# First pass of a vision tower: scan decays made in pairs of steps, hidden layers in two runs, norm roots and gate scratch in PSUM, routing two steps later

## The chip, the cores and the metric

The kernel runs on one core of a Trainium2 chip, as one launch. The time is device time in microseconds (us), the median of several runs of the same program. The core has five engines that run at once and wait for each other by semaphores: TensorE (PE, with its weight loads, PEld), VectorE (DVE), ScalarE (ACT), GpSimd (POOL) and SyncE (SP, which here only issues transfers). SBUF is the on-chip memory of 128 partitions, PSUM the small one of eight banks that PE's products are written to.

## What is computed

32 images of 96x96 become 38 tokens each of 192 features: 36 patches and two class tokens. Two layers follow, each a state-space scan and a mixture of experts, both with a residual. Cut to what matters here, the first layer:

```
def mlp(x, w1, b1, w2, b2): return silu(x @ w1 + b1) @ w2 + b2

x = layernorm(h)                            # tokens x 192
a = -abs(mlp(x, A...)); b = mlp(x, B...); c = mlp(x, C...)      # 16 states each
delta = sigmoid(mlp(x, d...)); dt = exp(log_dt)                 # 192 each
# along the tokens of an image, for each feature and state:
state = (delta * state + (1 - delta) * x * b * dt) * exp(a * dt)
y = sum over states(state * c) + x * D
h = h + y
logits = layernorm(h) @ Wr.T                # 8 experts
top 2 of 8, weights = softmax of the two
h = h + sum over the two: weight * (gelu(x @ Wi[e].T + bi[e]) @ Wo[e].T + bo[e])
```

The second layer has two selective scans (forward and backward) between a projection down and one up, and a second mixture whose gates are chosen in the same way.

## The kernel before

The images are cut into four groups of eight, so T = 304 token columns. Features lie on partitions, 128 of them ("main", names ending in m) and 64 ("rest", ending in r). Some tensors pack both parts as PK = 456 columns, the rest's two halves of 152 columns under each other.

**Three stages.** The first pass does the first layer's scan and the routing of its experts; 34 expert blocks follow (they begin while the last group is scanned); the second pass does the second layer. The change lies in the first pass, and in two helpers that the second pass uses too.

**The first pass** is software pipelined. A body (s, p, m) scans group s, prepares group p and routes group m, and the program runs six: (none, 0, none), (0, 1, none), (1, 2, 0), (2, 3, 1), (3, none, 2), (none, none, 3). Each body has twelve steps n = 0 to 11 (QSTEPS), and for every engine a function `first(s, p, m)` says by hand what it does in step n: the order of work is that of the code, and engines meet by semaphores alone. In the text p and m are also the groups' buffers (p_Xm is group p's normed main part; m's centred parts lie in q_Cm and q_Cr).

**Scan of s**, one step for each of twelve slices of states and features, tiles of 128x608: SP loads decays dA and b rows BB into a ring of four slots; ACT makes the exponentials `exp(a*dt)` with `p_decay` (L996, two of 304 columns) into a ring EXq of EXPS = 3 buffers, two steps ahead (AHEAD); POOL multiplies dA by them (L719); DVE does the b product into PSUM (L1298), the c product (L1311) and the scan (L1319); POOL multiplies scan and c product (L725); PE sums that over states (`first_sum`). The c product of step c waits for the sum of step c - 3 (ring PR3). At the end of a body the states C, A and B of the next group come from PE's `states` and ACT (L1070 to L1075).

**Preparing p**: `patches` and `tokens` make the tokens (class columns copied on DVE, L1350, patches added, L1352). `centre` takes the mean off (L1202, L1203), ACT squares (L880, L882), PE's `variance` sums them, `rstd` makes the root as logarithm (L887) and exponential (L892) into RS, and DVE's `scale` multiplies (L1207, L1208). Eleven hidden layers follow (PE, then a silu on ACT, L921), in order 3, 3, 3, 2 over steps 2 to 5; the first two belong to the delta. ACT's `delta` makes the sigmoid (L1013, L1015). Then DVE's `first_scan_input` (step 5):

```
OM = -1 * DL + 1                                  # L1363
WV = (OM * dt0) * UP, main and rest apart         # L1365
DL[first token of each image] = 0, then signal w_ready
base = x * D0 + h, three parts                    # L1369
```

UP is a copy of x made by ACT (L1058 to L1060).

**Routing m**: mean, variance, root and scale as above (scale at step 4), logits on PE and ACT, `gates_top` (step 8) picks the two best experts with comparisons and maxima of 102x24 (L1224 to L1238), `ranks` on PE counts the tokens before each one, `route` and `give_slots` (step 9) make weights and slots (L1264 to L1280), POOL scatters the rows to their slots. After groups 1 and 3 `make_table` (L1498 to L1521, step 10) makes the table of expert blocks. The scratch of the gates lies in SBUF (m_gate, m_gs, KEEP). ACT loads a table of functions each time it changes between the silu, the sigmoid and the exponential/logarithm (ACT_TABLE_LOAD).

**Queues of the transfers.** SP's queue has the ring's loads in order of the steps, the stores of the group before and, in the scan of group 3, from step 4 on, the weights and rows of the first expert blocks. These also wait for the table and for the scatters of POOL's queue.

**The second pass** norms and chooses gates with the same `scale`, `gates_top` and `gates_weights` (L1242 to L1256).

## Time and profile before

| | |
|---|---|
| median of 3 runs | 945.74 us (945.5 to 946.44) |
| the profiled execution | 946.11 us, span 944.3 us |
| mean granted TensorE clock | 0.899 of full speed |
| busy, share of the span | PE 741.0 us (78%), PEld 62%, DVE 576.6 (61%), ACT 404.1 (43%), POOL 386.8 (41%) |
| instructions | 11558 |
| first bodies | 0 to 54 us prepare group 0 and load constants |
| scans of groups 0, 1, 2 | 54 to 108, 108 to 175, 175 to 247 us |
| scan of group 3, with the first expert blocks | from 247 us |
| second pass | from 534 us |

How to read it: a share of busy time is a mean over stages that have different limits. A stretch says how busy each engine was in it; the groups by line say how long one instruction of a kind takes and how long its engine stood idle just before it, with the instruction that ended that idle time; the timeline lists single instructions with their start. Busy time of PE is modelled. Three views can show the same microsecond: an idle time of DVE is also a busy or an idle time of the engine it waits for.

### The profile page before, as it was taken

How to read it: one execution, taken by the hardware profiler on the slowest of the kernel's cores; microseconds unless marked ns; L12 is line 12 of the kernel's file. 1: busy time of each engine (PE TensorE's matmuls, PEld its weight loads, DVE VectorE, ACT ScalarE, POOL GpSimd, SP SyncE). 2: the span in 40 equal slices, each digit the busy share in tenths (PEclk: the TensorE clock that was granted, in tenths of full speed). 3: DMA queues.
4: the chain of work that ended last, by engine and by line, in shares of the span. 5: the costliest groups of instructions: out<-in, count | busy, mean ns of one | idle time of the engine just before them, and what ended most of it. 6: DMA issues, size and time to landing. Idle time of an engine off the chain costs nothing. (4 is left out here: it accounts for less than half of the span.)

```text
span 944.3 us, 11558 instructions
## 1 busy us (share of the span) xinstructions
PE 741.0 (78%) x3622; PEld 585.7 (62%) x3622; DVE 576.6 (61%) x994; ACT 404.1 (43%) x875; POOL 386.8 (41%) x305
## 2 busy tenths in 40 slices
PE   7877888685547869877999677888886997787688
PEld 5645656454327869877898545666664775565455
DVE  4167779679765532312111387899796859777835
ACT  1549275374233324422245373644724455355120
POOL 1045745655672411303003144654366433653430
PEclk9899999798677989999999888888977999899899
DMA  9469755355494658888677597787679565967600
GB/s 353 128 205 343 228 154 152 91 136 142 127 266 113 185 170 242 254 258 232 191 241 223 152 233 190 195 220 189 158 201 252 151 168 143 268 167 187 195 1 21
DMA packets 84067, 177.66 MB, mean 188 GB/s; under 512 B 12671, under 2 KB 32357, under 8 KB 83365
## 3 DMA queue, kind: packets, MB, share of 16 engines
q1 hardware_dynamic: 79172, 169.67, 63.6%
q0 software_dynamic: 4832, 7.24, 2.6%
q8 instruction: 29, 0.48, 0.2%
q14 instruction: 34, 0.27, 0.1%
HBM read 156.15 MB, written 20.69 MB: 187 GB/s over the span
## 5 line engine op out<-in xcount | busy, mean ns | idle before, releaser
L1759 PE MATMUL PS<-PR,CM 128*128 128x304 f32 (+1 forms) x672 | 186.8, 420 | 92.3 <-POOL PR L806 63.2
L806 POOL TENSOR_TENSOR PR<-ST,V 128x608 f32<-128x608 f32 x96 | 142.4, 1483 | 185.5 <-DVE ST L1340 153.8
L1759 PEld LDWEIGHTS PS<-PR,CM 128*128 128x128 f32 x672 | 126.8, 221 | 134.7 <-POOL PR L806 76.8
L976 ACT ACTIVATE dA<-dA,negA 128x304 f32<-128x304 f32 x192 | 93.7, 540 | 151.3 <-DMA BB<-rows_d 151.1
L1340 DVE TENSOR_TENSOR_SCAN ST<-dA,PS 128x608 f32<-128x608 f32 x96 | 136.4, 1420 | 15.1 <-ACT dA L976 11.0
L1028 ACT ACTIVATE HID<-PS,WX 128x128 f32<-128x128 f32 x204 | 59.6, 367 | 150.0 <-PE PS L1759 149.9
L719 POOL TENSOR_TENSOR dA<-dA,aP 128x607 f32<-128x607 f32 x48 | 70.7, 1474 | 71.5 <-ACT aP L996 69.7
L1536 DVE TENSOR_TENSOR xp<-PS,WXB 128x192 f32<-128x192 f32 x34 | 12.2, 358 | 127.0 <-PE PS L1759 127.0
L1329 DVE TENSOR_TENSOR PS<-BB,PS 128x608 f32<-128x608 f32 x96 | 76.2, 794 | 21.5 <-DMA BB<-rows_d 10.7
L1759 PE MATMUL PS<-XT,WX 128*128 128x128 f32 x408 | 83.3, 288 | 1.0 <-ACT HID L1028 1.0
L1759 PE MATMUL PS<-XT,WXR 128*128 128x128 f32 x408 | 83.0, 287 | 0.0
L734 POOL DMA_DIRECT2D outs_d<-xp x34 | 19.5, 573 | 147.9 <-DVE xp L1536 147.9
L1759 PE MATMUL PS<-WX,HID 128*128 128x192 f32 x408 | 74.1, 331 | 7.3 <-DVE XT L1529 7.3
L1759 PEld LDWEIGHTS PS<-WX,HID 128*128 128x128 f32 x408 | 67.5, 194 | 8.2 <-issue 4.8
L725 POOL TENSOR_TENSOR PR<-PR,ST 128x608 f32<-128x608 f32 x32 | 47.2, 1474 | 59.4 <-DVE ST L1319 59.3
L1319 DVE TENSOR_TENSOR_SCAN ST<-dA,PS 128x608 f32<-128x608 f32 x48 | 67.8, 1413 | 2.5 <-POOL dA L719 1.8
L1759 PEld LDWEIGHTS PS<-XT,WX 128*128 128x128 f32 x408 | 66.4, 204 | 1.2 <-ACT HID L1028 1.2
L1759 PEld LDWEIGHTS PS<-XT,WXR 128*128 128x128 f32 x408 | 66.0, 204 | 0.0
L1759 PE MATMUL PS<-HB,CM 96*128 96x152 f32 (+1 forms) x240 | 48.8, 355 | 0.2 <-ACT HB L1130 0.2
L1759 PEld LDWEIGHTS PS<-HB,CM 96*128 96x128 f32 x240 | 40.1, 204 | 8.1 <-issue 3.1
L1759 PE MATMUL PS<-p_Xm,WX 128*128 128x304 f32 x88 | 32.8, 456 | 14.5 <-ACT HID L921 11.6
L1298 DVE TENSOR_TENSOR PS<-BB,PS 128x608 f32<-128x608 f32 x48 | 38.0, 792 | 9.3 <-ACT PS L1075 7.1
(380 smaller groups left out, 1318.6 us busy)
## 6 DMA issues: line engine op xcount, KB each, us to landing
dA<-rows_d SPq DMA_DIRECT2D x144, 304.0 KB, 4.4
BB<-rows_d SPq DMA_DIRECT2D x144, 304.0 KB, 5.1
WX<-ex_m SPq DMA_DIRECT2D x34, 576.0 KB, 4.0
WX<-ex_m SPq DMA_DIRECT2D x34, 387.0 KB, 3.8
slots_d<-WXR SPq DMA_DIRECT2D x8, 960.0 KB, 8.8
WXR<-ex_r SPq DMA_DIRECT2D x34, 192.0 KB, 4.9
CM<-c SPq DMA_DIRECT2D x1, 4430.0 KB, 19.6
WX<-gates_d SPq DMA_DIRECT2D x3, 1216.0 KB, 6.6
```

The lines of the kernel that those rows point to most:

```text
L719: nc.gpsimd.tensor_tensor(now[:, 1:], now[:, 1:], before[:, 0:QB * T - 1], ALU.mult).then_inc(ap_ready.sem, 1)
L725: nc.gpsimd.tensor_tensor(PR3[c % 3], PR3[c % 3], STq[:, c % 2], ALU.mult).then_inc(P.product.sem, 1)
L734: pool.dma_start(outs_d[b // HALF_BLOCKS][at:at + 128, :], YB[:, b % 3, :]).then_inc(out_rows[b % 3], 16)
L806: nc.gpsimd.tensor_tensor(PRq[:, c % 2], STq[:, c % 2], DIRS[k].Cw.unsqueeze(1).broadcast_to([128, QB, T]), ALU.mult).then_inc(q_product.s ...
L976: last = nc.scalar.activation(dAq[:, slot, i, :], dAq[:, slot, i, :], ACT.Exp, scale=negA[:, j:j + 1])
L1028: last = nc.scalar.activation(HX[:, p, f, :], PS[:, wide_bank(b, h), j * 128:(j + 1) * 128], ACT.Gelu, bias=WX[:, p, FFN + f:FFN + f + 1])
L1298: nc.vector.tensor_tensor(BPq[0], BBq[:, slot], PS[:, B1_BANK, 0:T].unsqueeze(1).broadcast_to([128, QB, T]), ALU.mult).then_inc(P.b_times_ ...
L1319: nc.vector.tensor_tensor_scan(flat(STq[:, c % 2], False), flat(dAq[:, slot], False), BP[0], 0.0, ALU.mult, ALU.add).then_inc(P.scanned.se ...
L1329: nc.vector.tensor_tensor(BPq[k], BBq[:, slot], BW[k].unsqueeze(1).broadcast_to([128, QB, T]), ALU.mult).then_inc(b_times_w.sem, 1)
L1340: nc.vector.tensor_tensor_scan(flat(STq[:, c % 2], back), flat(dAq[:, slot], back), BP[k][:, ::-1] if back else BP[k], 0.0, ALU.mult, ALU. ...
L1536: nc.vector.tensor_tensor(YB[:, p, :], PS[:, SHARED_BANK, 256:256 + D], WXB[:, p, :], ALU.add).then_inc(y_copied.sem, 1)
L1759: return nc.tensor.matmul(out, lhsT, rhs, start=first, stop=last)
```

## The change

**Buffers.** EXPS becomes 6. The three new buffers of the decays lie over buffers that only the second pass uses: two in q_DL_OM_WV (DL, OM and WV of the second pass) and one in p_OM_TM; group p keeps DL and WV apart.

**Order on ACT.** In a middle body the decays come in pairs of steps (DECAYS_AT), those of steps 0 and 1 still at the end of the body before. Squares and root of p come ahead of the step's decays. The hidden layers come in two runs, 0 to 5 and 6 to 10, with the delta between them and no decays within a run.

**Delta.** ACT scales UP by dt0 as it copies. Beside the sigmoid DL it makes 1 - delta as sigmoid(-x - b), into the PSUM bank that holds the delta's product. DVE's `first_scan_input` multiplies UP by that bank: one product of 456 columns in the place of OM and two.

**Roots and gates.** `rstd` writes the root into the PSUM bank of the variance (except for one norm, L), and `scale` reads it there. The scratch of the gates lies in the same bank (`choice_views`); the copy of the logits goes, copies of the second choice and of the first weight come.

**Class tokens** are copied for group 0 only; the buffers keep them.

**Routing** comes later where a group is prepared in the same body (`routed_at`): scale of m at step 6 for 4, logits 7 for 5, transposed logits 8 for 7, gates 9 for 8, route and slots 10 for 9, the table 11 for 10. POOL's scatters follow.

**Order on PE.** The variance of p comes before the sum of step 0, layers 0 and 1 before the mean of m, the delta's product after four layers, and at the end of a body the states B before the sum of step 10. Patches and token rows wait for WV (w_ready) instead of the delta.

The core of the diff:

```diff
-SLOTS, AHEAD, EXPS = 4, 2, 3
+SLOTS, AHEAD, EXPS = 4, 2, 6
+DECAYS_AT = {0: (2, 3), 1: (4, 5), 2: (6, 7), 4: (8, 9), 6: (10, 11)}
...
+        def routed_at(n, p):
+            if p is None or n <= 3:
+                return n
+            return {6: 4, 7: 5, 8: 7, 9: 8, 10: 9, 11: 10}.get(n)
...
             def rstd(s, g, bank):
                 act.wait_ge(s.ln_var.sem, s.ln_var.after(g, 1))
                 log_of(s, 128, bank, s.ln_log)
-                power_of(s, 128, s.ln_log, s.ln_rstd, g, 1)
+                power_of(s, 128, s.ln_log, s.ln_rstd, g, 1, None if s is L else PS[:, bank, 0:T])
...
-                nc.scalar.activation(P.DL[:, T:PK], PS[:, MEAN_BANK, T:PK], ACT.Sigmoid, bias=cm("d_b2", 1, 2)).then_inc(delta_ready.sem, 1)
+                nc.scalar.activation(P.DL[:, T:PK], PS[:, MEAN_BANK, T:PK], ACT.Sigmoid, bias=cm("d_b2", 1, 2))
+                for h, cols in enumerate(MAIN_REST):
+                    tables[0] = None
+                    last = nc.scalar.activation(PS[:, MEAN_BANK, cols], PS[:, MEAN_BANK, cols], ACT.Sigmoid, bias=neg_db2[:, h:h + 1], scale=-1.0)
+                last.then_inc(delta_ready.sem, 1)
...
+                    for c in DECAYS_AT.get(n, ()) if s is not None else ():
+                        p_decay(s, c)
...
-                            nc.scalar.activation(P.UP[:, 0:T], P.Xm[:, :], ACT.Copy)
+                            nc.scalar.activation(P.UP[:, 0:T], P.Xm[:, :], ACT.Copy, scale=dt0[:, 0:1])
...
-                        if n == 4:
-                            hidden(p, 6, 9)
                         if n == 5:
-                            hidden(p, 9, 11)
+                            hidden(p, 6, 11)
...
-            def scale(s, g, li):
+            def scale(s, g, li, bank):
                 dve.wait_ge(s.ln_rstd.sem, s.ln_rstd.after(g, li + 1))
-                nc.vector.tensor_tensor(s.Xm[:, :], s.Cm[:, :], s.RS[:, :], ALU.mult)
+                nc.vector.tensor_tensor(s.Xm[:, :], s.Cm[:, :], PS[:, bank, 0:T], ALU.mult)
...
+            def choice_views(bank):
+                each = TILES * EXPERTS
+                wide = [PS[0:TW, bank, T + j * each:T + (j + 1) * each].rearrange("p (t e) -> p t e", e=EXPERTS) for j in range(6)]
...
-                link(s, g, nc.vector.tensor_copy(L, PS[0:TW, bank, 0:TILES * EXPERTS].rearrange("p (t e) -> p t e", e=EXPERTS)))
...
+                    link(s, g, nc.vector.tensor_copy(oh2, picked))
...
-                    nc.vector.tensor_copy(hv[:, :, 0:2], cm(cls, p=rows).unsqueeze(1).broadcast_to([rows, IMG, 2]))
+                    if g == 0:
+                        nc.vector.tensor_copy(hv[:, :, 0:2], cm(cls, p=rows).unsqueeze(1).broadcast_to([rows, IMG, 2]))
...
-                link(P, g, nc.vector.tensor_scalar(P.OM[:, :], P.DL[:, :], -1.0, 1.0, ALU.mult, ALU.add))
-                for h, cols in enumerate(MAIN_REST):
-                    nc.vector.scalar_tensor_tensor(P.WV[:, cols], P.OM[:, cols], dt0[:, h:h + 1], P.UP[:, cols], ALU.mult, ALU.mult)
+                nc.vector.tensor_tensor(P.WV[:, :], P.UP[:, :], PS[:, MEAN_BANK, 0:PK], ALU.mult)
...
-                    pe.wait_ge(delta_ready.sem, delta_ready.after(p - 1, 1))
+                    pe.wait_ge(P.w_ready.sem, P.w_ready.after(p - 1, 1))
```

**ACT, the first steps of the body that scans group 1.** Before (L996 decays, L880 and L882 squares of p, L887 and L892 its root, L859 and L921 table loads, HID and HIDr the silus, aP the ring of decays):

```order
L880 ACTIVATE p_RS<-p_Cm 128x304
L882 ACTIVATE p_SQr<-p_Cr 64x304
L996 ACTIVATE aP<-q_R,neg_dtq 128x304 x2
L887 ACTIVATE p_VE<-PS,eps_col 128x304
L892 ACTIVATE p_RS<-p_VE 128x304
L996 ACTIVATE aP<-q_R,neg_dtq 128x304 x2
L921 ACT_TABLE_LOAD
L921 ACTIVATE HID<-PS,WX 128x304
L921 ACTIVATE HIDr<-PS,WX 64x304
L921 ACTIVATE HID<-PS,WX 128x304
L859 ACT_TABLE_LOAD
L996 ACTIVATE aP<-q_R,neg_dtq 128x304 x2
```

With the change (L1009 decays, L893 and L895 squares, L900 and L905 the root, now into PS; q_DL_OM_WV and p_OM_TM are the new buffers of the ring):

```order
L893 ACTIVATE p_RS<-p_Cm 128x304
L895 ACTIVATE p_SQr<-p_Cr 64x304
L1009 ACTIVATE aP<-q_R,neg_dtq 128x304 x2
L1009 ACTIVATE q_DL_OM_WV<-q_R,neg_dtq 128x304 x2
L900 ACTIVATE p_VE<-PS,eps_col 128x304
L905 ACTIVATE PS<-p_VE 128x304
L1009 ACTIVATE q_DL_OM_WV<-q_R,neg_dtq 128x304 x2
L1009 ACTIVATE p_OM_TM<-q_R,neg_dtq 128x304 x2
L1009 ACTIVATE aP<-q_R,neg_dtq 128x304 x4
L934 ACT_TABLE_LOAD
L934 ACTIVATE HID<-PS,WX 128x304
L934 ACTIVATE HIDr<-PS,WX 64x304
```

The decays of step 3 and those of steps 4 to 7 stand around the root, then no exponential until the delta is done; two loads between the first silus are gone.

**ACT, the delta of the same body.** Before (L1013 and L1015 the sigmoid):

```order
L859 ACT_TABLE_LOAD
L996 ACTIVATE aP<-q_R,neg_dtq 128x304 x2
L887 ACTIVATE q_VE<-PS,eps_col 128x304
L892 ACTIVATE q_RS<-q_VE 128x304
L1058 ACTIVATE p_UP<-p_Xm 128x304
L1059 ACTIVATE p_UP<-p_Xr 64x152
L1060 ACTIVATE p_UP<-p_Xr 64x152
L1013 ACT_TABLE_LOAD
L1013 ACTIVATE p_DL<-PS,WX 128x304
L1015 ACTIVATE p_DL<-PS,WX 128x152
L921 ACT_TABLE_LOAD
L921 ACTIVATE HID<-PS,WX 128x304 x3
```

With the change (L1060 to L1062 UP scaled by dt, L1026 and L1028 the sigmoid, L1031 that of the negated product; L934 and L871 table loads):

```order
L934 ACTIVATE HID<-PS,WX 128x304 x3
L1060 ACTIVATE p_UP<-p_Xm,dt 128x304
L1061 ACTIVATE p_UP<-p_Xr,dt 64x152
L1062 ACTIVATE p_UP<-p_Xr,dt 64x152
L1026 ACT_TABLE_LOAD
L1026 ACTIVATE p_DL<-PS,WX 128x304
L1028 ACTIVATE p_DL<-PS,WX 128x152
L1031 ACTIVATE PS<-PS,neg_db 128x304
L1031 ACTIVATE PS<-PS,neg_db 128x152
L871 ACT_TABLE_LOAD
L900 ACTIVATE q_VE<-PS,eps_col 128x304
L905 ACTIVATE PS<-q_VE 128x304
```

The delta comes after six layers as before, with nothing but silus ahead of it, and the root of m, which stood ahead of the delta, now follows it.

**PE, where the body that scans group 1 begins.** Before (HID,WX the states C, then B; PR,CM and V,CM sums over states; p_RS and p_SQr the variance of p; m_Hm, m_Hr the mean of m; p_Xm, p_Xr a hidden layer):

```order
L1759 MATMUL PS<-HID,WX 128x304 x3
L1759 MATMUL PS<-PR,CM 128x152 x4
L1759 MATMUL PS<-HID,WX 128x304 x3
L1759 MATMUL PS<-V,CM 128x152 x4
L1759 MATMUL PS<-PR,CM 128x304 x2
L1759 MATMUL PS<-p_RS,ones_d 128x304
L1759 MATMUL PS<-p_SQr,ones_d 128x304
L1759 MATMUL PS<-PR,CM 128x304 x2
L1759 MATMUL PS<-m_Hm,ones_d 128x304
L1759 MATMUL PS<-m_Hr,ones_d 128x304
L1759 MATMUL PS<-p_Xm,WX 128x304
L1759 MATMUL PS<-p_Xr,WX 128x304
```

With the change:

```order
L1785 MATMUL PS<-HID,WX 128x304 x6
L1785 MATMUL PS<-PR,CM 128x152 x4
L1785 MATMUL PS<-V,CM 128x152 x4
L1785 MATMUL PS<-p_RS,ones_d 128x304
L1785 MATMUL PS<-p_SQr,ones_d 128x304
L1785 MATMUL PS<-PR,CM 128x304 x4
L1785 MATMUL PS<-p_Xm,WX 128x304
L1785 MATMUL PS<-p_Xr,WX 128x304
L1785 MATMUL PS<-p_Xm,WX 128x304
L1785 MATMUL PS<-p_Xr,WX 128x304
L1785 MATMUL PS<-m_Hm,ones_d 128x304
L1785 MATMUL PS<-m_Hr,ones_d 128x304
```

The states B follow C at once, ahead of the last two sums of group 0; the variance of p stands ahead of the sums of steps 0 and 1, and two hidden layers ahead of the mean of m.

## Rows read from the trace of the kernel before

**Rows 1.** Busy time in four stretches, headed us, engines busy (xinstructions), PEclk, DMA share, GB/s.

```profile
54.30:107.70 53.40, 41.38 (x158) 29.45 (x157) 41.18 (x52) 32.97 (x56) 32.83 (x23) 0.94 0.85 301
...
107.70:174.50 66.80, 52.04 (x220) 38.23 (x219) 52.58 (x83) 35.60 (x64) 37.18 (x27) 0.90 0.51 140
...
174.50:246.70 72.20, 45.93 (x190) 33.63 (x189) 55.98 (x94) 35.60 (x64) 42.86 (x32) 0.82 0.46 123
...
277.60:534.20 256.60, 218.34 (x1527) 206.51 (x1526) 76.99 (x248) 91.22 (x252) 62.27 (x71) 0.93 0.70 206
```

**Rows 2.** DVE's costliest groups, 54 to 285 us: xcount | busy us, mean ns | idle before, releasers.

```profile
L1207 DVE TENSOR_TENSOR p_Xm<-p_Cm,p_RS 128x304 f32<-128x304 f32 x3 | 1.5, 508 | 11.6 <-ACT p_RS L892 11.6
...
L1207 DVE TENSOR_TENSOR m_Xm<-q_Cm,q_RS 128x304 f32<-128x304 f32 x3 | 5.9, 1953 | 11.4 <-ACT q_RS L892 11.4
...
L1298 DVE TENSOR_TENSOR PS<-BB,PS 128x608 f32<-128x608 f32 x43 | 34.0, 792 | 9.2 <-ACT PS L1075 7.1
...
L1266 DVE TENSOR_TENSOR KEEP<-m_gs,KEEP 102x3 f32<-102x3 f32 x2 | 2.7, 1326 | 0.1
...
L1276 DVE TENSOR_TENSOR m_gate<-KEEP,m_gate 102x24 f32<-102x24 f32 x2 | 2.5, 1240 | 0.0
...
L1365 DVE SCALAR_TENSOR_TENSOR p_WV<-p_OM,dt,p_UP 128x304 f32<-128x304 f32 x3 | 3.8, 1264 | 0.1
...
L1363 DVE TENSOR_SCALAR p_OM<-p_DL 128x456 f32<-128x456 f32 x3 | 1.1, 375 | 3.8 <-ACT p_DL L1015 3.8
...
L1350 DVE COPY p_Hr<-WX 64x16 f32<-64x16 f32 x2 | 2.4, 1218 | 0.0
```

**Rows 3.** Timeline of DVE, 146 to 163 us: start us, us, engine, line, operation, out<-in.

```profile
146.14 0.80 DVE L1298 TENSOR_TENSOR PS<-BB,PS 128x608 f32<-128x608 f32 x1
...
149.06 0.80 DVE L1298 TENSOR_TENSOR PS<-BB,PS 128x608 f32<-128x608 f32 x1
...
152.68 1.07 DVE L1228 TENSOR_TENSOR m_gate<-m_gate,m_gs 102x24 f32<-102x24 f32 x1
...
153.78 1.40 DVE L1229 TENSOR_TENSOR m_gate<-m_gate,CM 102x24 f32<-102x24 f32 x1
...
155.43 1.18 DVE L1231 TENSOR_TENSOR KEEP<-m_gate,m_gs 102x24 f32<-102x24 f32 x1
...
157.08 0.18 DVE L1228 TENSOR_TENSOR m_gate<-m_gate,m_gs 102x24 f32<-102x24 f32 x1
...
162.49 0.17 DVE L1273 TENSOR_TENSOR m_gate<-PS,run 102x24 f32<-102x24 f32 x1
```

**Rows 4.** Timeline of POOL at 153 us.

```profile
153.67 1.48 POOL L725 TENSOR_TENSOR V<-V,ST 128x608 f32<-128x608 f32 x1
```

**Rows 5.** Timeline of PE, three places.

```profile
106.95 1.20 PE L1759 MATMUL PS<-PR,CM 128*128 128x152 f32 x8
...
115.68 1.22 PE L1759 MATMUL PS<-p_RS,ones_d 128*128 128x304 f32 x2
...
159.90 3.16 PE L1759 MATMUL PS<-xp,WX 128*128 128x288 f32 x12
```

**Rows 6.** Timeline of ACT, 119 to 125 us.

```profile
119.86 1.28 ACT L921 ACT_TABLE_LOAD   x1
...
124.21 0.51 ACT L921 ACTIVATE HIDr<-PS,WX 64x304 f32<-64x304 f32 x1 [0.51 <-PE PS L1759]
```

**Rows 7.** Timeline of DVE, end of the body of group 2.

```profile
234.82 0.14 DVE L1498 TENSOR_TENSOR counts<-run,CM 102x8 f32<-102x8 f32 x1
...
241.13 0.16 DVE L1521 CAST tab_rows<-block_f 1x17 int32<-1x17 f32 x1
...
246.69 0.79 DVE L1311 TENSOR_TENSOR PR<-aP,PS 128x608 f32<-128x608 f32 x1 [2.69 <-ACT PS L1073]
...
250.24 0.80 DVE L1298 TENSOR_TENSOR PS<-BB,PS 128x608 f32<-128x608 f32 x1 [2.76 <-ACT PS L1075]
```

**Rows 8.** DVE's groups, second pass, 530 to 900 us.

```profile
L1255 DVE TENSOR_TENSOR q_gate<-q_gate,q_gs 102x24 f32<-102x24 f32 x3 | 2.7, 902 | 0.1
```

More of the change, by code:

```diff
@@ L138, in vit_tower @@
         dt0 = sb("dt0", [128, 2])
+        neg_db2 = sb("neg_db2", [128, 2])
         neg_dtq = sb("neg_dtq", [128, FEAT_BLOCKS])
@@ L750, in first @@
                         first_product(s, c)
-                    if m and c in (1, 2, 3, 4):
+                    begun = 1 if p is not None or s == GROUPS - 1 else 2
+                    if m and begun <= c + 1 < len(pieces):
                         scatter(m - 1, *pieces[c + 1])
@@ L754, in first @@
                         scatters_done(m - 1)
-                    if m is not None and c == 10:
+                    first_at = 10 if p is None else 11
+                    if m is not None and c == first_at:
                         pool.wait_ge(s_zero, 128)
@@ L759, in first @@
                         pool.sem_inc(turn_taken, 1)
-                    if m is not None and c in (10, 11):
-                        for t, k in (pieces[c - 10:c - 9] if s is not None else pieces if c == 10 else ()):
+                    if m is not None and c >= first_at:
+                        for t, k in (pieces[c - first_at:c - first_at + 1] if s is not None else pieces if c == 10 else ()):
                             scatter(m, t, k)
@@ L1033, in first @@
                 for n in range(QSTEPS):
-                    if s is not None and n + AHEAD < QSTEPS:
-                        p_decay(s, n + AHEAD)
-                    elif p is not None and n + AHEAD >= QSTEPS:
-                        p_decay(p, n + AHEAD - QSTEPS)
+                    if p is not None:
+                        if n == 0:
+                            squares(P, p, 0)
+                        if n == 1:
+                            rstd(P, p, MEAN_BANK)
+                        if n == (3 if s is None else 4):
+                            act.wait_ge(P.ln_x.sem, P.ln_x.after(p, 1))
+                            if s is not None:
+                                act.wait_ge(P.w_ready.sem, P.w_ready.after(s, 1))
+                            nc.scalar.activation(P.UP[:, 0:T], P.Xm[:, :], ACT.Copy, scale=dt0[:, 0:1])
+                            nc.scalar.activation(P.UP[0:DR, T:PK], P.Xr[:, 0:HALF], ACT.Copy, scale=dt0[0:DR, 1:2])
+                            nc.scalar.activation(P.UP[DR:128, T:PK], P.Xr[:, HALF:T], ACT.Copy, scale=dt0[DR:128, 1:2]).then_inc(packed_x.sem, 1)
+                            delta(s, p)
                     if m is not None:
@@ L2054, in first @@
                         first_sum(m, QSTEPS - 1)
-                    if s is not None and 0 < n < QSTEPS - 1:
-                        first_sum(s, n - 1)
                     if n == 1:
@@ L2106, in first @@
                         states(p, 1, B1_BANK).then_inc(b1_mm.sem, 1)
-                    if n == 3 and m is not None:
-                        variance(M, m, 0, ROUTE_BANK)
+                    if s is not None and n == QSTEPS - 1:
+                        first_sum(s, n - 1)
                     b = block_now(s, p, n)
```

156 lines of the change are left out of this document (82 added, 74 removed).

## Prediction

> **What bounds the kernel now.** I read the busy time by stretch first. The three stretches from 54.3 to 246.7 us are the bodies of the first pass that scan groups 0, 1 and 2: 53.4, 66.8 and 72.2 us [rows 1], 192.4 together. No engine fills them: DVE, the busiest, has 41.18 + 52.58 + 55.98 = 149.7 us, ACT and POOL far less. So the bodies are paid for by DVE's work and by what DVE waits for. A scan step alone needs 149.06 - 146.14 = 2.92 us of DVE [rows 3], twelve of them 35 us; a body's other 18 to 37 us are what the change can reach. The stretch of expert blocks behind them has PE busy 218.34 of 256.6 us [rows 1] and gets none of the change.
>
> Next DVE's groups in the first pass, the idle column first. DVE waits 11.6 us for the root of the norm of the group being prepared (p), 11.4 us for that of the routed group (m), 3.8 us for the delta, and 7.1 of the 9.2 us ahead of the b products for the states B1 [rows 2]. Then the duration column: a product of 128x304 took 0.508 us for p and 1.953 for m; products of three columns took 1.326 [rows 2].
>
> The timelines tell why the same operation has two durations. At 152.68 a comparison of 24 columns took 1.07 us, its successor 1.40; at 157.08 the same line took 0.18 [rows 3]. At 153.67 POOL began a product of 1.48 us [rows 4]. The long ones have both inputs in SBUF and lie beside a POOL operation; at 162.49 an addition with one input in PSUM took 0.17 beside other long ones [rows 3]. So I read the excess as time behind POOL's operation, for pairs of SBUF inputs only. The trace has no changed operation, so this is an inference.
>
> **The change, part by part**, against the profiled execution's 946.1 us (0.4 above the median shown).
>
> What goes:
> - Wait for p's root, 11.6 [rows 2]. Today PE sums step 0, which needs POOL's product, before the variance; the variance now comes first, and DVE has two scan steps (5.8 us) to cover squares, products and root. All of it is counted; at worst none.
> - Wait for m's root, 11.4 [rows 2]. The scaling moves from step 4 to step 6 and follows WV. On ACT the root now stands a load (1.28 [rows 6]) and about 1 us of root behind the delta; DVE has after the delta WV, the scan's additions (about 1.8 together) and one scan step, 4.7 us. So it is hidden, and shows only where ACT takes twice as long.
> - The same scaling no longer has two SBUF inputs: (1.953 - 0.508) x 3 = 4.3 [rows 2].
> - Gates: 1.07 + 1.40 + 1.18 - 3 x 0.18 = 3.1 a group [rows 3], two groups beside a scan: 6.2. Route and slots: (1.326 + 1.240 - 2 x 0.17) x 2 = 4.5 [rows 2, 3]. The two copies that are added cost 0.2 each and replace one.
> - WV: one product instead of one OM and two more. From 0.17 us at 24 columns and 0.508 at 304 I estimate 0.69 at 456 columns: (1.264 - 0.69) x 3 = 1.7, OM 1.1 [rows 2, 3]: 2.8. The second product is counted at nothing.
> - Copies of class tokens: 2.4 [rows 2]; those of the other tensor are left to the upper bound.
> - B1 before the last sum: a sum of eight products takes 1.20 us [rows 5], its successor starts about 1.0 later; two boundaries, 2.0. At the third the table of blocks (241.13 + 0.16 - 234.82 = 6.5 us of DVE) moves behind step 11, between that step and the waits for C1 and B1, 2.69 + 2.76 = 5.4 [rows 7]; it covers them both.
> - Today's wait for the delta, 3.8 [rows 2].
>
> Sum: 11.6 + 11.4 + 4.3 + 6.2 + 4.5 + 2.8 + 2.4 + 2.0 + 5.4 + 3.8 = 54.4.
>
> What comes:
> - Two more sigmoids, each near 0.51 like a silu of ACT [rows 6]: 1.0, in the body that only prepares group 0, where nothing covers them.
> - The delta, in two bodies. Counted from the body's first product, DVE has scaled p after about 7.5 us: B1 (1.5), two steps, the scaling. From there ACT needs 2.1 to the first silu (two layers' pace), six layers at 1.02 (0.51 of work, 0.51 of wait [rows 6]) 6.1, behind mean M and a sum 2.4, delta's products 1.5, UP 1.0, load 1.3, four sigmoids 1.6: 23.5 together, 24 with a wait between. DVE has the old output of m (1.0), four steps (11.7), a centring (0.8) and a wait for mean M (1.4): 22.4. I take 1.5 x 2 = 3.0; bounds 0 and 3.8 x 2.
> - Mean M now stands on PE behind layers 0 and 1. Two layers are 2.0 us at the pace of rows 6, twice that at half the clock: for the variance PE took 1.22 us for 608 columns where a sum had 1216 in 1.20 [rows 5]. I take 1.4 where group 0 is routed and 3.0 where group 1 is: 4.4; bounds 0 and 6.
> - The sum of step 5 stands on PE behind layers 8 to 10. These wait for the second run of silus, which has behind the delta a load (1.28), a root (1.0), four exponentials (1.9) and another load: 28.9 us, with five layers 34.0, with the sum 35.2. DVE wants it for the product of step 8 at about 32.6 (delta 23.5, WV and additions 1.8, two steps, the scaling of m 0.8, a b product 0.7). 2.6 us in one body; 0.2 in group 0's. 2.8; bounds 0 and 7.8.
> - Ranks come behind the second half of the patches (3.16 [rows 5]) and one sum (1.20): at most 4.4 later. I take 3.4, in the body where DVE has nothing else to wait for; bounds 0 and 8.8.
> - Smaller ones without a row of their own, 5.6: patches that wait for WV instead of the delta (2.0), logits behind the moved scaling, scan additions that now meet a POOL operation (2.6), the decays in the body of group 3 (1.0). Bounds 0 and 11.6, what one kind of root wait costs today.
>
> Sum: 1.0 + 3.0 + 4.4 + 2.8 + 3.4 + 5.6 = 20.2.
>
> The decays in pairs and four table loads fewer per body (5.1 us of ACT [rows 6]) count for nothing by themselves: ACT is busy 35.60 of 66.8 us [rows 1]. They pay for the earlier delta and root above. POOL's and SP's work in the scan is the same; scatters move one step later and end before the blocks ask for rows.
>
> The net is 54.4 - 20.2 = 34.2. The expert blocks start from loads that SP issues after step 4 of group 3's scan, so they shift as a whole. In the second pass the gates have one long line, (0.902 - 0.18) x 3 = 2.2 [rows 3, 8], half of it counted: 1.1. That gives 946.1 - 35.3 = 910.8, about **911 us**.
>
> One rule speaks against the change. A PSUM input of 24 columns took 0.17 us and an SBUF pair 0.18 [rows 3], so moving operands is priced at nothing. The Trainium skill (VectorE: DVE Perf Modes, The TRN2 errata) gives VectorE 58 fixed cycles from SBUF to SBUF and 120 from PSUM, at 0.96 GHz, from which I estimate 65 ns more for each moved operation. The trace does not agree for these sizes.
>
> **The rivals.**
> - *New waits eat most of it.* For it: the new queue orders put delta, sums and ranks in a row, and each term above is bounded at about twice its value. Against it: DVE's old waits are measured, and each is removed by order alone. Costs at twice: 946.1 - 15.1 = 931. Chance 0.15.
> - *No new wait.* The orders were read too strictly, and what DVE meets late is covered. 946.1 - 55.5 = 891. Against it: sigmoids and ranks can hardly hide. 0.04.
> - *PSUM operands are dear.* If each moved operation, some 25 a group and 100 in all, cost the whole of a short one again, 0.17 [rows 3], the gain would shrink by 17 us: 928. Against it the two rows named above. 0.03. By the 65 ns of the Trainium skill (VectorE: DVE Perf Modes, The TRN2 errata) it would be 917.5.
> - *The gain does not reach the end*: the blocks wait for something with its own time, a DMA, whose share is 0.70 there [rows 1]. What stays is 1.1: 945, no change. Against it: their loads are issued by order. 0.03.
> - *Slower: the clock.* The granted clock fell to 0.82 in the body with the longest waits [rows 1]. If two runs of layers with a gap leave PE at 1.2 GHz in all of them, a layer takes 1.02 us more and the delta's products as much as 1.5 layers: 12.5 x 1.02 x 3 = 38.2, so 949. It turns the sign only past 37.2, that is if nearly every layer runs so and none is hidden. Against it: shorter waits keep PE busier. 0.03.
>
> **How the numbers follow.** The forecast, 901 to 920 (costs between half and one and a half times 20.2), has 0.72. A difference of 0.2%, 1.9 us, is about what a measurement of this kernel can tell. Faster: 0.72 + 0.15 + 0.04 + 0.03 = 0.94; same 0.03; slower 0.03. The range for 8 in 10 adds some of the first two rivals: 898 to 929.
>
> **What would show it.** In the first pass of the changed kernel the two root waits should be below 1 us each; scaling m near 0.5 us; no gate operation over 0.3 us; the bodies of groups 0, 1 and 2 near 49, 58 and 56 us. New waits should stand ahead of WV, mean M, the c product of step 8 and the slots. It is wrong if the gates stay at 1.0 to 1.4 us though in PSUM, if DVE waits over 5 us for the delta in a body, or if the stretch of the blocks grows by what the bodies lose.

## The result, and the profile after

The changed kernel took 922.73 us (median of 4 runs, 922.23 to 925.4), the kernel before 945.7: ratio 0.9735, interval 0.9704 to 0.9766, so 23.0 us less. A second set of runs beside the experiments gave 0.9699 (0.9658 to 0.9739). The forecast was 911 with a range of 898 to 929: the sign is right, the time lies in the range, but above the narrower 901 to 920 that had the chance of 0.72; the gain is two thirds of the 35 forecast, and it does not come from where the prediction had it.

The busy time by stretch of the changed kernel, the scans of groups 0, 1 and 2 and then that of group 3 up to the fifth expert block, answers to [rows 1] (us, busy of PE, PEld, DVE, ACT, POOL, then PEclk, DMA share, GB/s):

```profile
55.50:107.60 52.10, 42.92 (x155) 30.63 (x155) 38.90 (x47) 28.39 (x55) 33.00 (x23) 0.87 0.88 309
...
107.60:171.10 63.50, 52.62 (x219) 39.55 (x219) 44.24 (x79) 31.27 (x62) 35.91 (x26) 0.87 0.56 146
...
171.10:235.20 64.10, 49.39 (x210) 37.16 (x209) 51.64 (x93) 33.95 (x69) 45.39 (x34) 0.84 0.55 145
...
235.20:295.30 60.10, 40.98 (x207) 32.30 (x208) 40.31 (x77) 19.11 (x45) 35.35 (x26) 0.80 0.75 205
```

For the expert blocks a row of DVE serves as a mark, the copy that begins the fifth block: at 320.01 us before, at 295.33 after. With it the span falls into these stretches:

| us | before | forecast | after |
|---|---|---|---|
| up to the first c product of group 0 | 54.3 | 55.3 | 55.5 |
| scan of group 0 | 53.4 | 49 | 52.1 |
| scan of group 1 | 66.8 | 58 | 63.5 |
| scan of group 2 | 72.2 | 56 | 64.1 |
| scan of group 3 to the fifth block | 73.3 | about 67 | 60.1 |
| from there to the end of the span | 624.3 | 623 | 625.6 |

The prediction names the three bodies; its 67 and 623 are what its sum leaves for the rest. The three bodies gave 12.7 us where 29 were forecast; the scan of group 3 gave 13 where 6 were. What comes behind moved as a whole; the 1.3 us there are no more than executions differ by (from the second pass's first scan to the end it took 401 to 408 us in all of them, whatever the kernel).

DVE's groups in the first pass, 45 to 285 us, answer to [rows 2] (xcount | busy us, mean ns | idle before, releasers):

```profile
L1224 DVE TENSOR_TENSOR p_Xm<-p_Cm,PS 128x304 f32<-128x304 f32 x3 | 1.3, 446 | 0.0
...
L1224 DVE TENSOR_TENSOR m_Xm<-q_Cm,PS 128x304 f32<-128x304 f32 x3 | 1.3, 445 | 0.0
...
L1253 DVE TENSOR_TENSOR PS<-PS,CM 102x24 f32<-102x24 f32 x6 | 1.1, 191 | 0.2
...
L1219 DVE TENSOR_TENSOR q_Cm<-m_Hm,PS 128x304 f32<-128x304 f32 x3 | 1.4, 471 | 14.0 <-PE PS L1785 14.0
...
L1393 DVE TENSOR_TENSOR p_WV<-p_UP,PS 128x456 f32<-128x456 f32 x3 | 1.9, 630 | 8.7 <-ACT PS L1031 8.7
...
L1340 DVE TENSOR_TENSOR V<-aP,PS 128x608 f32<-128x608 f32 x8 | 6.3, 784 | 8.4 <-PE PS L1785 8.3
...
L1340 DVE TENSOR_TENSOR V<-p_OM_TM,PS 128x608 f32<-128x608 f32 x7 | 5.5, 780 | 1.4 <-PE PS L1785 1.4
...
L1327 DVE TENSOR_TENSOR PS<-BB,PS 128x608 f32<-128x608 f32 x46 | 36.4, 792 | 4.9 <-ACT PS L1092 2.2 <-DMA BB<-rows_d 0.4
...
L1397 DVE SCALAR_TENSOR_TENSOR q_TM<-p_Xm,WX,p_Hm 128x304 f32<-128x304 f32 x2 | 4.5, 2259 | 0.0
```

Both root waits are gone, to the last tenth. Scaling m takes 445 ns for 1953, and a comparison of the gates (L1253) 191 ns where two of four took over 1 us. But DVE now waits 14.0 us for the mean of the routed group, 8.7 for the delta and 8.4 + 1.4 for sums ahead of c products; before, it was 2.4, 3.8 and none. (In a second execution of the changed kernel the three are 10.7, 8.7 and 9.7 us, so the wait for the mean varies by 3.)

The body of group 1 on DVE's timeline, only its longer waits (mean, delta, sum ahead of the product of step 8, ranks):

```profile
123.34 0.47 DVE L1219 TENSOR_TENSOR q_Cm<-m_Hm,PS 128x304 f32<-128x304 f32 x1 [4.49 <-PE PS L1785]
...
135.00 0.63 DVE L1393 TENSOR_TENSOR p_WV<-p_UP,PS 128x456 f32<-128x456 f32 x1 [2.25 <-ACT PS L1031]
...
147.82 0.79 DVE L1340 TENSOR_TENSOR V<-aP,PS 128x608 f32<-128x608 f32 x1 [3.80 <-PE PS L1785]
...
163.63 0.17 DVE L1292 TENSOR_SCALAR PS<-m_gs 102x3 f32<-102x3 f32 x1 [4.32 <-PE PS L1785]
```

### The profile page after: what moved, and what is told of

Same layout as the page of the kernel before. It is cut to its first block and busy times, and to the rows that moved or that the text cites. A ratio compares the mean times of both kernels' runs of the same rounds, so it can differ in the third digit from the quotient of the medians.

```text
span 920.9 us, 11542 instructions
## 1 busy us (share of the span) xinstructions
PE 739.0 (80%) x3622; PEld 584.5 (63%) x3622; DVE 548.9 (60%) x980; ACT 388.7 (42%) x870; POOL 386.9 (42%) x305
## 5 line engine op out<-in xcount | busy, mean ns | idle before, releaser
L1785 PE MATMUL PS<-PR,CM 128*128 128x304 f32 (+1 forms) x672 | 183.2, 414 | 82.5 <-POOL PR L818 59.8
L1785 PEld LDWEIGHTS PS<-PR,CM 128*128 128x128 f32 x672 | 124.3, 218 | 124.4 <-POOL PR L818 72.8
L1358 DVE TENSOR_TENSOR PS<-BB,PS 128x608 f32<-128x608 f32 x96 | 76.2, 794 | 22.3 <-DMA BB<-rows_d 11.2
L735 POOL TENSOR_TENSOR PR<-PR,ST 128x608 f32<-128x608 f32 x32 | 47.2, 1474 | 63.5 <-DVE ST L1348 63.5
L729 POOL TENSOR_TENSOR dA<-dA,aP 128x607 f32<-128x607 f32 x24 | 35.3, 1474 | 49.3 <-ACT aP L1009 45.5
L1785 PE MATMUL PS<-p_Xm,WX 128*128 128x304 f32 x88 | 39.3, 536 | 20.4 <-ACT HID L934 18.5
L1785 PE MATMUL PS<-WX,CM 128*128 128x304 f32 x144 | 41.5, 423 | 0.4 <-POOL WX L826 0.4
```

Source lines behind the costliest of these rows:

```text
L729: nc.gpsimd.tensor_tensor(now[:, 1:], now[:, 1:], before[:, 0:QB * T - 1], ALU.mult).then_inc(ap_ready.sem, 1)
L735: nc.gpsimd.tensor_tensor(PR3[c % 3], PR3[c % 3], STq[:, c % 2], ALU.mult).then_inc(P.product.sem, 1)
L1358: nc.vector.tensor_tensor(BPq[k], BBq[:, slot], BW[k].unsqueeze(1).broadcast_to([128, QB, T]), ALU.mult).then_inc(b_times_w.sem, 1)
L1785: return nc.tensor.matmul(out, lhsT, rhs, start=first, stop=last)
```

## The experiments

Each kernel ran beside the kernel before on the same chip. The ratios have intervals of 0.3 to 0.5% to each side, so small differences are also read from the traces: from the first c product of group 0 to the fifth block it is 265.7 us before, and 239.8 and 235.4 in two executions of the changed kernel.

**The changed kernel again.**

> The changed kernel itself once more, beside the others of this call: ratio to the kernel before 0.9735 within its interval.

0.9699 (0.9658 to 0.9739). What this execution adds is the body of group 1: 59.5 us in the place of 63.5, by the same program. The row answers to the second one above:

```profile
110.50:170.00 59.50, 48.63 (x219) 37.21 (x219) 44.22 (x80) 31.26 (x62) 35.63 (x26) 0.94 0.56 157
```

PE's timeline in this body, the sum of step 1 and the first products of layer 0, in the first execution and in this one:

```profile
116.01 2.39 PE L1785 MATMUL PS<-PR,CM 128*128 128x304 f32 x4 [1.63 <-POOL PR L735]
...
118.20 1.22 PE L1785 MATMUL PS<-p_Xm,WX 128*128 128x304 f32 x2
```

```profile
118.90 1.29 PE L1785 MATMUL PS<-PR,CM 128*128 128x304 f32 x4 [1.63 <-POOL PR L735]
...
120.03 0.68 PE L1785 MATMUL PS<-p_Xm,WX 128*128 128x304 f32 x2
```

PE waited for POOL in the same way (1.63 us), but then the sum took 2.39 us in the one and 1.29 in the other, a pair of the layer 1.22 and 0.68. The granted clock over the body was 0.87 and 0.94, DVE's wait for the mean 4.49 and 1.55 us, its other waits alike within 0.8. So some 3 us of this body go with PE's clock alone.

**The mean ahead of hidden layers 0 and 1 again, as it was before the change.**

```diff
+                        if m is not None:
+                            pe.wait_ge(scan_out.sem, scan_out.after(m, 1))
+                            mean(M, M, m, 0, ROUTE_BANK)
                         if p is not None:
                             pe.wait_ge(P.ln_x.sem, P.ln_x.after(p, 1))
-                            hidden(p, 0, 1)
...
-                            hidden(p, 1, 2)
...
-                            hidden(p, 2, 4)
+                            hidden(p, 0, 4)
```

> The changed kernel with the mean of the routed group back ahead of hidden layers 0 and 1 on PE. Theory A (one chain: in a body that prepares a group, everything up to WV lasts as long as the chain norm, hidden layers, delta on PE and ACT, so DVE's wait for the mean and its wait for the delta are one budget): the waits for the mean in the bodies of groups 1 and 2 (4.5 and 5.8 us) fall below 2, the waits for the delta (2.25, 2.1) grow by nearly as much, and the time stays within 3 us of the changed kernel's 922.7. Theory B (the waits add up): the mean's waits go and nothing comes, about 914.

0.9694 (0.9649 to 0.9739), 921.7 us: no change. DVE's waits for the mean and for the delta in the body of group 1:

```profile
120.34 0.47 DVE L1219 TENSOR_TENSOR q_Cm<-m_Hm,PS 128x304 f32<-128x304 f32 x1 [1.61 <-PE PS L1785]
...
134.82 0.63 DVE L1393 TENSOR_TENSOR p_WV<-p_UP,PS 128x456 f32<-128x456 f32 x1 [4.34 <-ACT PS L1031]
```

The wait for the mean fell from 4.49 to 1.61 us and that for the delta rose from 2.25 to 4.34; WV began 27.3 us behind the body's first product, and 27.4 in the changed kernel. In group 2's body the wait for the mean fell only from 5.84 to 2.97, the one for the delta rose from 2.14 to 4.34, and WV began after 28.7 us in both. Theory A holds: what DVE waits for ahead of WV is one budget, set by the chain of the norm, the layers and the delta on PE and ACT.

**The sum of step 1 behind layers 0, 1 and the mean.**

```diff
-                    if s is not None and 0 < n < QSTEPS - 1:
+                    if s is not None and 0 < n < QSTEPS - 1 and not (n == 2 and p is not None):
                         first_sum(s, n - 1)
...
                             mean(M, M, m, 0, ROUTE_BANK)
                         if p is not None:
+                            if s is not None:
+                                first_sum(s, 1)
                             hidden(p, 2, 4)
```

> The changed kernel with the sum of step 1 behind hidden layers 0, 1 and the mean on PE, in the place of ahead of them. Theory A (the chain to the delta bounds, and that sum, which waits for POOL, stands in it): layer 0 starts 2 to 3 us earlier in three bodies, delta too, so 6 to 9 us less: 914 to 917. Theory B (waits add up; DVE names no wait for that sum): no change, 921 to 924.

0.9595 (0.9543 to 0.9647), 909.1 us; from the first product to the fifth block 230.0 us. It beats both kernels, by more than the 6 to 9 us of theory A. PE in the body of group 2, first in the changed kernel (sums of steps 0 and 1, then layer 0 and the mean):

```profile
176.59 1.29 PE L1785 MATMUL PS<-PR,CM 128*128 128x304 f32 x4 [1.40 <-POOL PR L735]
...
180.87 2.39 PE L1785 MATMUL PS<-PR,CM 128*128 128x304 f32 x4 [2.99 <-POOL PR L735]
...
183.06 1.22 PE L1785 MATMUL PS<-p_Xm,WX 128*128 128x304 f32 x2
...
186.97 0.68 PE L1785 MATMUL PS<-m_Hm,ones_d 128*128 128x304 f32 x2
```

DVE had the scaled p ready by 178.6. PE then waited 2.99 us for POOL's product of step 1, ran its sum in 2.39 us, and came to layer 0 at 183.06, at 1.22 us for a pair. The granted clock from 179 to 189 us was 0.66 of full speed, so part of it ran at 1.2 GHz and part at 2.4. With the sum moved (layer 0, then the sum):

```profile
174.86 0.78 PE L1785 MATMUL PS<-p_Xm,WX 128*128 128x304 f32 x2 [0.75 <-DVE p_Xr L1225]
...
178.03 1.19 PE L1785 MATMUL PS<-PR,CM 128*128 128x304 f32 x4
```

Layer 0 follows DVE's scaling at once, 7.5 us behind the body's first product in the place of 11.9, a pair takes 0.68 us (the first 0.78), the sum 1.19, and the clock from 175 to 185 us was 1.00. The bodies of groups 0, 1 and 2 reach WV after 24.4, 25.2 and 23.5 us; in the two executions of the changed kernel it was 25.1 and 26.2, 27.4 and 24.4, 28.7 and 28.5. So in group 2's body the sum in the chain cost 5 us, the half pace of PE behind its wait included; in group 1's it cost what the clock made of it, 2.2 us in one execution and nothing in the other.

**Gate scratch back in SBUF.** `gates_top`, `gates_weights`, `route` and `give_slots` as before, the rest changed.

> The changed kernel with the scratch of the gates, of route and of the slots back in SBUF (the copy of the logits with it). If operations with two SBUF inputs wait for POOL's product: those at 0.18 us go back to 1.0 to 1.4 us, 3.1 us for the gates and 2.2 for route and slots in each of groups 0 to 2, 16 in sum, less the 4.3 that DVE waits for the ranks of group 0: 934 to 939. If the later place or the copies made them short: not over 3 us more, below 926.

0.9778 (0.9729 to 0.9826), 930.1 us: between the two, 4 to 7 us above the changed kernel's two ratios, whose intervals it overlaps, and 7 to 12 us by the trace (247.1 us to the fifth block). Operations of groups 0 (the first two) and 1 on DVE's timeline:

```profile
155.35 1.43 DVE L1253 TENSOR_TENSOR m_gate<-m_gate,CM 102x24 f32<-102x24 f32 x1
...
164.66 0.18 DVE L1300 TENSOR_TENSOR m_gate<-KEEP,m_gate 102x24 f32<-102x24 f32 x1
...
225.51 1.24 DVE L1300 TENSOR_TENSOR m_gate<-KEEP,m_gate 102x24 f32<-102x24 f32 x1
```

POOL's products at these three places:

```profile
155.24 1.50 POOL L729 TENSOR_TENSOR dA<-dA,p_OM_TM 128x607 f32<-128x607 f32 x1
...
163.09 1.47 POOL L729 TENSOR_TENSOR dA<-dA,aP 128x607 f32<-128x607 f32 x1
...
225.24 1.46 POOL L729 TENSOR_TENSOR dA<-dA,aP 128x607 f32<-128x607 f32 x1
```

So the wait behind POOL's product ("the lock" of the expectations) is real, and the trace shows which operation it hits. L1253 started 0.11 us after a product of POOL and ended with it, L1300 of group 1 started 0.27 us after one and ended with it; L1300 of group 0 started 0.10 us after one had ended (163.09 + 1.47) and took 0.18. In the changed kernel, with an input and the output in PSUM, the same L1253 took 0.19 us in the middle of a product of POOL:

```profile
154.14 0.19 DVE L1253 TENSOR_TENSOR PS<-PS,CM 102x24 f32<-102x24 f32 x1
```

```profile
153.00 1.47 POOL L735 TENSOR_TENSOR PR<-PR,ST 128x608 f32<-128x608 f32 x1
```

The three bodies took 180.3 us, where the changed kernel took 179.7 and 175.3; the wait for the ranks fell from 4.32 to 1.20 us at the same time. What was lost lies for the most part in the scan of group 3, 66.8 us for 60.1, where four operations of group 2's gates and weights took 0.95 to 1.86 us, together 4.9 us above 0.14 to 0.18 each. The price was put too high because most of the operations fell between POOL's products.

**The kernel before with roots and gate scratch in PSUM, nothing else.**

```diff
-                power_of(s, 128, s.ln_log, s.ln_rstd, g, 1)
+                power_of(s, 128, s.ln_log, s.ln_rstd, g, 1, None if s is L else PS[:, bank, 0:T])
...
-                nc.vector.tensor_tensor(s.Xm[:, :], s.Cm[:, :], s.RS[:, :], ALU.mult)
+                nc.vector.tensor_tensor(s.Xm[:, :], s.Cm[:, :], PS[:, bank, 0:T], ALU.mult)
...
+                L, (q, picked, _, _, _, _), (m2, _, _, _) = choice_views(bank)
```

> The kernel before with norm roots and gate scratch in PSUM and nothing else: every order as it was. By the lock: scaling m 4.3 us, gates 9.3, route and slots 6.7, 1 in the second pass: 21 less, 925, and the waits for the two roots stay at 11 each; the new order is then worth next to nothing. If the order earns the larger part: 938 to 943.

0.9866 (0.9814 to 0.9918), so 13 us less than before: short of the 21, about half of the change. To the fifth block it is 256.8 us, 8.9 less. The root waits stay, as expected (p's and m's, group 1's body):

```profile
118.59 0.47 DVE L1207 TENSOR_TENSOR p_Xm<-p_Cm,PS 128x304 f32<-128x304 f32 x1 [3.56 <-ACT PS L892]
...
135.25 0.47 DVE L1207 TENSOR_TENSOR m_Xm<-q_Cm,PS 128x304 f32<-128x304 f32 x1 [5.65 <-ACT PS L892]
```

**Decays one step at a time in the changed kernel.**

```diff
-                    for c in DECAYS_AT.get(n, ()) if s is not None else ():
-                        p_decay(s, c)
+                    if s is not None and n + AHEAD < QSTEPS:
+                        p_decay(s, n + AHEAD)
```

> The changed kernel with the decays made one step at a time again, two steps ahead, the ring of 6 and all else kept. As the prediction priced them (worth nothing by themselves): within 2 us of the changed kernel. If the pairs pay: exponentials return between layers 2 and 3, two loads of 1.28 us and 1 us of work, so the delta comes up to 3.6 us later in three bodies, 6 to 10 us; and between the gelus of the expert blocks beside the scan of group 3, where the changed kernel gained 7 us, 5 to 7 us: 11 to 17 us more in sum.

0.9894 (0.985 to 0.9938), 939.2 us: the part that the prediction priced at nothing carries 15 to 18 us in the changed kernel. The three bodies took 54.6, 62.1 and 67.2 us, the scan of group 3 to the fifth block 68.8 where the changed kernel has 60.1. WV does not come later (26.1, 25.0 and 28.2 us after a body's first product), so the late delta that was expected is not the cost. DVE now waits for the exponentials themselves, which stand behind the run of silus:

```profile
96.16 0.79 DVE L1340 TENSOR_TENSOR V<-aP,PS 128x608 f32<-128x608 f32 x1 [3.62 <-ACT aP L1009]
...
150.60 0.79 DVE L1340 TENSOR_TENSOR V<-aP,PS 128x608 f32<-128x608 f32 x1 [3.19 <-ACT aP L1009]
```

Beside the blocks lies the other half. First ACT's timeline of the kernel before, between two gelus of the blocks (L1028): loads of tables, decays (L996) and a copy of token rows (L1079). Then the changed kernel, with the same copy (L1096):

```profile
295.27 0.88 ACT L1028 ACTIVATE HID<-PS,WX 128x128 f32<-128x128 f32 x3 [1.70 <-PE PS L1759]
...
296.17 1.28 ACT L859 ACT_TABLE_LOAD   x1
...
297.47 0.99 ACT L996 ACTIVATE aP<-q_R,neg_dtq 128x304 f32<-128x304 f32 x2
...
298.36 0.47 ACT L1079 ACTIVATE m_ACC<-PS 102x384 f32<-102x384 f32 x1
...
300.02 1.28 ACT L1028 ACT_TABLE_LOAD   x1
```

```profile
278.11 0.88 ACT L1045 ACTIVATE HID<-PS,WX 128x128 f32<-128x128 f32 x3 [1.70 <-PE PS L1785]
...
278.87 0.50 ACT L1096 ACTIVATE m_ACC<-PS 102x384 f32<-102x384 f32 x1
```

A load, two exponentials and a load back stood between two gelus, and in the run with single steps they stand there again. PE's wait for the copy, in that run and in the changed kernel:

```profile
288.57 0.47 PE L1785 MATMUL PS<-CM,m_Xm 128*102 128x128 f32 x2 [2.62 <-ACT m_ACC L1096]
```

```profile
279.42 0.46 PE L1785 MATMUL PS<-CM,m_Xm 128*102 128x128 f32 x2 [0.33 <-ACT m_ACC L1096]
```

In the kernel before it was 2.62 us too.

**The kernel before with decays in pairs, nothing else.**

```diff
-SLOTS, AHEAD, EXPS = 4, 2, 3
+SLOTS, AHEAD, EXPS = 4, 2, 6
+DECAYS_AT = {0: (2, 3), 1: (4, 5), 2: (6, 7), 4: (8, 9), 6: (10, 11)}
...
-                    if s is not None and n + AHEAD < QSTEPS:
-                        p_decay(s, n + AHEAD)
+                    for c in DECAYS_AT.get(n, ()) if s is not None else ():
+                        p_decay(s, c)
```

> The kernel before with the decays in pairs of steps and the ring of 6, nothing else (OM is written over WV, since the ring takes its buffer). If the pairs are a part of their own (taking them out of the changed kernel cost 18 us): 14 to 18 less than the kernel before. If they pay only together with the new orders, since DVE here still waits for both roots: 3 to 7 less.

0.9895 (0.9851 to 0.9938), 10 us less: between the two. To the fifth block it is 254.6 us, 11.1 less than before; 6.8 of them lie in the scan of group 3.

**The kernel before with both, pairs and PSUM, and no order changed.**

> The kernel before with decays in pairs, norm roots and gate scratch in PSUM; the orders of hidden layers, delta, PE and routing as they were. If the two parts add up (13 measured for PSUM, 14 to 18 for the pairs): 27 to 31 less than before, which is the whole change and more, and the new orders are worth nothing. If they overlap and the orders earn the rest: 15 to 20 less.

0.9713 (0.9659 to 0.9767), 919.4 us: 27 us less, the whole change within the interval. The two parts add up (13 + 10 = 23). To the fifth block it is 245.2 us, where the changed kernel has 239.8 and 235.4, so all the new orders together (hidden layers in two runs, delta, variance and B1 first, later routing, one product for WV) are worth at most 5 to 10 us by the trace, and nothing measurable in the whole time. The trace probably overstates them: this profiled execution took 926.3 us, 7 above its kernel's median, those of the changed kernel 922.9 and 923.6, 0 and 3 above theirs. And none of the 5 to 10 us lies in the three bodies that most of the orders were made for, which took 176.0 us here, 179.7 and 175.3 in the changed kernel; all of it lies in the scan of group 3, 69.2 us against 60.1 in both executions. There DVE waits 2.69 and 2.63 us for the states C1 and B1 at the start, the changed kernel for neither, and the first block begins 40.6 us after the first product, for 33.3 there. In this kernel DVE still waits for the root of m in the body of group 1, and at the first block of group 3:

```profile
131.03 0.47 DVE L1210 TENSOR_TENSOR m_Xm<-q_Cm,PS 128x304 f32<-128x304 f32 x1 [4.27 <-ACT PS L895]
...
271.48 0.29 DVE L1543 COPY XT<-PS 128x128 f32<-128x128 f32 x1 [11.81 <-PE PS L1990]
```

**Routing at its old steps in the changed kernel.** `routed_at` returns n, and POOL's scatters and ACT's logits follow.

> The changed kernel with the routing at its old steps (scaling m at step 4, gates 8, slots 9, table 10). If the later steps pay: ACT makes the root of m behind the delta, so DVE waits for it at step 4, about 2.3 us past the delta, and has the scaling and step 5 still ahead of WV: 4 to 6 us in the bodies of groups 1 and 2, less up to 4 for the ranks: 4 to 8 us more than the changed kernel. If not: within 2 us of it.

0.9774 (0.9726 to 0.9822), 925.9 us; 241.9 us to the fifth block. Both lie on the side expected, 4 to 7 us above the changed kernel in ratio, but the intervals overlap. The wait for m's root is there, in the bodies of groups 1 and 2 alike:

```profile
136.67 0.47 DVE L1222 TENSOR_TENSOR m_Xm<-q_Cm,PS 128x304 f32<-128x304 f32 x1 [7.45 <-ACT PS L903]
```

WV came later by it, after 30.2 us in the body of group 1 and 32.9 in that of group 2. Yet the body of group 1 took 58.2 us, less than in the changed kernel (63.5 and 59.5), since the wait for the ranks fell to 0.55 us; that of group 2 took 67.4 (64.1 and 63.8). So the later routing is not shown to pay.

**The sum of step 5 ahead of layers 8 to 10.**

```diff
-                    if s is not None and 0 < n < QSTEPS - 1:
+                    if s is not None and 0 < n < QSTEPS - 1 and not (n == 6 and p is not None):
                         first_sum(s, n - 1)
...
                         if n == 5:
+                            if s is not None:
+                                first_sum(s, 5)
                             hidden(p, 8, 11)
```

> The changed kernel with the sum of step 5 ahead of hidden layers 8 to 10 on PE. If those layers alone hold it up: DVE's waits before the c product of step 8 (3.0, 3.8 and 1.5 us) go, 5 to 8 us less. If DVE only comes earlier to the next late thing (the logits, the ranks, the sum of step 6): the waits move there, within 2 us of the changed kernel.

0.9717 (0.9683 to 0.9751), 920.9 us: no change. The wait moved one step on, to the product of step 9, which wants the sum of step 6 from behind the same layers. Layer 8 as PE of the changed kernel begins it in group 1's body, and the new wait of DVE:

```profile
140.92 1.38 PE L1785 MATMUL PS<-p_Xm,WX 128*128 128x304 f32 x2 [5.33 <-ACT HID L934]
```

```profile
149.45 0.79 DVE L1340 TENSOR_TENSOR PR<-q_DL_OM_WV,PS 128x608 f32<-128x608 f32 x1 [3.31 <-PE PS L1785]
```

**Three places of PE's order: sum 1, sum 5, ranks ahead of the second half of the patches.**

> The changed kernel with the sum of step 1 behind the mean of the routed group, the sum of step 5 ahead of layers 8 to 10 and the ranks ahead of the second half of the patches, on PE alone. If each of the three is a place of its own in the chain: 10 (as measured for the first) + 5 to 8 + 2 to 4 less than the changed kernel, 900 to 906. If the first has already taken what there was: 906 to 913.

0.9577 (0.9543 to 0.9611), 908.2 us. The wait for the ranks fell from 4.32 to 0.38 us, yet it is no faster than with sum 1 alone beyond the intervals: as the second theory had it.

**The sum of step 6 ahead of those layers too.**

> As the version with three places of PE's order changed (sum 1, sum 5, ranks), with the sum of step 6 ahead of layers 8 to 10 as well. If those layers keep up the sums one after the other: the waits ahead of the c product of step 9 (2.4, 2.6 us) go, 903 to 906. If what follows is late by itself (logits, states A): the wait moves there, 907 to 910.

0.966 (0.9611 to 0.9708), 913.6 us, above the version without it, though the two intervals touch. That is more than either theory had. The wait ahead of step 9 went in group 1's body (in group 0's it stayed, 2.45 us), the body of group 2 took 63.7 us for 58.4, and the wait moved on to the logits, which now come behind the later layers:

```profile
150.90 0.18 DVE L1251 TENSOR_REDUCE m_gs<-PS 102x3 f32<-102x24 f32 x1 [4.17 <-PE PS L1785]
...
211.11 0.18 DVE L1251 TENSOR_REDUCE m_gs<-PS 102x3 f32<-102x24 f32 x1 [5.38 <-PE PS L1785]
```

## Why the prediction was right and where it was wrong

*Longer operations beside POOL: right.* That pairs of SBUF inputs lose time to POOL and PSUM inputs do not was an inference; now it is shown by the kernel before with PSUM alone (13 us less) and by the gates back in SBUF (0.19 us becomes 1.43, and the operation ends with POOL's product). The terms for scaling, gates, route and slots were 15.0 us together, 16.1 with the second pass; the kernel before with PSUM alone measured 12.7 in the whole time and 8.9 to the fifth block. They were too high, since a freed DVE also comes earlier to the next wait (1.77 us for the ranks in the PSUM kernel). The additions of the scan's input still have two SBUF inputs, and took 2259 ns on average in the changed kernel, where one that met no wait took 562. The Trainium skill (SBUF — State Buffer, Who interferes with whom) says that between engines only the port pair shared by VectorE and GpSimd contends, as an exclusive lock. These rows agree. Only the prediction's "for pairs of SBUF inputs only" was too narrow, and its own rows had the sign: the copy of class tokens of 64x16, with one input, took 1.22 us on average [rows 2]. In the kernel before it took 1.29 us from 167.67 on, inside a product of POOL begun at 167.47, and the one before it, of 128x16, 0.15 us at 167.25 with POOL idle. The rival of dear PSUM operands falls: 191 ns with input and output in PSUM, 0.18 us in SBUF [rows 3].

*"All of it is counted", of the two root waits: this is the step that failed.* The waits went, 11.6 and 11.4 us, as forecast. But they stood ahead of WV, which needs the delta, and the interval from a body's first product to WV (before, to OM, which led to it) is set by the delta's own chain: 26.7, 32.1 and 33.0 us before, 25.1, 27.4 and 28.7 after. Where 23.0 us were booked, the three intervals together shrank by 10.6, and by 12.7 in the second execution. What DVE no longer waited for the roots it waited for the mean and the delta. The experiment on the mean shows it: 2.9 us of that wait taken away in the bodies of groups 1 and 2 brought neither WV nor the end forward. The prediction did work out the delta's chain, 23.5 to 24 us, and used it only for a term of 1.5 us per body. It left out of that chain PE's sum of step 1, which stands ahead of layer 0 and waits for POOL, and the clock at which PE leaves that wait. With the sum moved, the chain measures 24.4, 25.2 and 23.5, close to what had been worked out.

*The sizes of the new waits*, forecast and measured by DVE's idle time: mean M 4.4, but 14.0 - 2.4 = 11.6 (8.3 in the second execution); delta 3.0, but 8.7 (the 4.3 us of group 0's body stayed, and the 3.8 of today were booked as gone); sums ahead of c products 2.8, but 8.4 + 1.4 = 9.8; ranks 3.4 and 4.3; patches 2.0 and 2.1. Named rightly, they are 36 us together with these five in the place of 15.6. The price of sum 5 went wrong twice: PE had waited 5.33 us for the silu of layer 6 in group 1's body and ran layers 8 to 10 at half pace after it (1.38 us for the first pair), and every later sum stands behind the same layers, so there is nothing to win by moving one (the runs with sums 5 and 6).

*"The decays in pairs ... count for nothing by themselves": wrong.* The reason given was that ACT is busy half the time. That says nothing of what stands in its queue between two silus or two gelus. Alone the pairs brought 10 us, and in the changed kernel their loss cost 15 to 18, in part because the two runs of silus then hold up the decays. Much of this lies beside the expert blocks, where the prediction looked for no gain from them: of the 13 us by which the scan of group 3 became shorter, the pairs alone give 6.8, and their loss costs 8.7.

*The shift of the blocks: right.* The fifth block came 24.7 us earlier and the end 23.4.

So it is luck that the time fell into the range: two errors of opposite sign met, orders that earn nothing measurable (at most 5 to 10 us in single traces) where the sum gave them nearly 20, and a part at 10 us or more that had been priced at none. Of the rivals the one in which new waits eat most of the gain was nearest in its mechanism. With the sum of step 1 moved the orders do earn: 0.9595 (0.9543 to 0.9647), where pairs and PSUM without the orders gave 0.9713 (0.9659 to 0.9767). Moving that sum without the other orders was not run.

Open: what the new orders earn; the times leave some 6 us to either side of nothing, and the traces put it all into the scan of group 3. The single product for WV, the class tokens, B1 ahead of the last sum and the later table were not taken apart. Nor was the longer ring of decays run on the kernel before without the pairs; in the changed kernel the ring alone does not give what the pairs give, since it was kept when they were taken out.

## What to carry to other kernels

Waits of one engine ahead of the same operation are one budget: before removing one, find the chain that releases that operation, and price only what makes this chain shorter, each queued operation in it included. An engine's busy share does not price what stands in its queue: moving table loads out from between two dependent operations can pay on an engine that is half idle. To split a change of many parts, run the parts alone on the kernel before as well as taken out of the one after; here two lines of the change, PSUM operands and decays in pairs, gave the whole within the interval.
